# Adding the scan's carried states with one full-width product instead of four quarter-width products

## The reference, cut to what matters

```python
def step(h, inp):
    dt_t, B_t, C_t, x_t = inp
    dA = jnp.exp(dt_t[..., None] * A)
    h = dA * h + (dt_t * x_t)[..., None] * B_t[:, None, :]
    y = jnp.einsum('bdn,bn->bd', h, C_t)
    return (h, y)
h0 = jnp.zeros((B, D_INNER, D_STATE), xc.dtype)
_, ys = jax.lax.scan(step, h0, scan_xs)
```

## Time and profile before

| | us |
|---|---|
| median of 3 runs | 711.44 |
| lowest, highest | 710.73, 712.69 |
| the profiled execution, its own time | 711.19 |
| span of its instructions | 709.3 |
| TensorE busy in the span | 644.8 |
| VectorE, ScalarE, GpSimd busy | 551.7, 403.5, 385.7 |
| mean granted TensorE clock | 0.98 |

### The profile page before, as it was taken

One profiled execution on the slowest core, in us unless ns is written; L12 is line 12 of the kernel. 1 busy time (PEld: TensorE's weight loads), 2 busy tenths in 40 slices (PEclk: granted clock), 3 DMA queues, 4 the chain that ended last, 5 costly groups with the idle time before them and its releaser, 6 DMA issues.

```text
span 709.3 us, 25399 instructions
## 1 busy us (share of the span) xinstructions
PE 644.8 (91%) x11476; PEld 447.5 (63%) x11476; DVE 551.7 (78%) x466; ACT 403.5 (57%) x794; POOL 385.7 (54%) x140
## 2 busy tenths in 40 slices
PE   1989986999988999899999999999898999999997
PEld 1333342588977889788888889954345555565532
DVE  5599668489988989799899989963759787892345
ACT  1434789898877677677778767502247345324100
POOL 1000246779988789889899898963101143533000
PEclk9999999999999999999999999999989999999999
DMA  7980053420064110431340100015039899760202
GB/s 213 82 66 5 29 153 125 144 63 19 19 141 132 35 48 19 126 89 52 108 117 20 48 18 19 5 35 182 0 84 199 177 249 222 163 117 2 56 3 119
DMA packets 72627, 62.12 MB, mean 88 GB/s; under 512 B 34024, under 2 KB 57576, under 8 KB 72520
## 3 DMA queue, kind: packets, MB, share of 16 engines
q1 hardware_dynamic: 71560, 60.09, 36.9%
q10 hardware_dynamic: 960, 0.41, 0.2%
HBM read 44.22 MB, written 15.25 MB: 84 GB/s over the span
## 4 chain that ended last, share of the span: by engine, by line
PE 66%; POOL 11%; ACT 10%; DVE 7%; issue 4%; DMA 1%; SPq 0%; POOLq 0%; ACTq 0%; DVEq 0%
PE PS L1219 21%; PE PS L1338 8%; PE PS L1452 6%; POOL X L573 5%; PE PS L1241 5%; PE PS L1103 5%; PE PS L1436 4%; POOL arena L573 3%; POOL WIN L573 3%; PE PS L1267 2%; PE PS L1356 2%; PE PS L1238 2%; PE PS L1317 1%; ACT arena L837 1%; DMA X<-in_x 1%
## 5 line engine op out<-in xcount | busy, mean ns | idle before, releaser
L573 POOL TENSOR_TENSOR X<-X,spare 128x2048 f32<-128x2048 f32 x32 | 146.6, 4584 | 20.5 <-DVE X L1688 10.6
L1219 PE MATMUL PS<-mid,arena 128*32 128x128 f32 x4096 | 137.8, 273 | 6.6 <-issue 5.6
L1219 PEld LDWEIGHTS PS<-mid,arena 128*32 128x32 f32 x4096 | 121.6, 110 | 19.0 <-issue 13.2
L1219 PE MATMUL PS<-APROD,arena 128*32 128x128 f32 x2048 | 129.5, 273 | 3.1 <-issue 3.0
L1219 PE MATMUL PS<-WPR,arena 128*32 128x128 f32 x2048 | 128.9, 273 | 3.5 <-issue 1.3
L1219 PEld LDWEIGHTS PS<-WPR,arena 128*32 128x32 f32 x2048 | 110.7, 110 | 14.7 <-issue 6.9
L1219 PEld LDWEIGHTS PS<-APROD,arena 128*32 128x32 f32 x2048 | 111.2, 110 | 2.6 <-issue 2.2
L837 ACT ACTIVATE arena<-arena,small 128x512 f32<-128x512 f32 (+1 forms) x150 | 99.4, 711 | 18.4 <-DVE X L1688 10.0
L598 POOL TENSOR_TENSOR arena<-arena,PWR 128x512 f32<-128x512 f32 x30 | 42.7, 1454 | 70.6 <-PE PS L1338 70.5
L573 POOL TENSOR_TENSOR arena<-arena,spare 128x2048 f32<-128x2048 f32 x16 | 73.4, 4585 | 10.1 <-ACT mid L845 6.0
L573 POOL TENSOR_TENSOR WIN<-WIN,spare 128x2048 f32<-128x2048 f32 x16 | 73.3, 4583 | 7.1 <-DVE WIN L1688 5.0
(11 more groups left out here) (201 smaller groups left out, 1183.6 us busy)
## 6 DMA issues: line engine op xcount, KB each, us to landing
arena<-dt_rows SPq DMA_DIRECT2D x56, 256.0 KB, 3.8
arena<-patch_rows SPq DMA_DIRECT2D x40, 324.0 KB, 6.0
patch_rows<-arena SPq DMA_DIRECT2D x10, 648.0 KB, 7.2
X<-in_x SPq DMA_DIRECT2D x4, 1024.0 KB, 7.6
dt_rows<-arena SPq DMA_DIRECT2D x8, 512.0 KB, 2.6
spare<-c_rows SPq DMA_DIRECT2D x64, 64.0 KB, 2.2
tap_rows<-WPR SPq DMA_DIRECT2D x24, 88.0 KB, 7.7
mid<-dt_rows SPq DMA_DIRECT2D x8, 256.0 KB, 3.8
```

Of the source, the lines that this page charges most:

```text
L573: pool.tensor_tensor(HB[s % 4], HB[s % 4], CROW[:, k % 2:k % 2 + 1, :].broadcast_to([P, QN, HALF]), ALU.mult).then_inc(S["g_rd"], 1)
L1219: mm = pe.matmul(PS[32 * n:32 * n + 32, 4 + i, j * P:(j + 1) * P], DXT[:, DT_ * b + g, 4 * h + j, 32 * i:32 * i + 32], DIAGB[k % 2][n][:, ...
```

## The change

In every half-step with `h = 1`, the four quarter-width products at line 1223 become one product with the whole 128-column identity as the stationary operand, into all 128 partitions of the same column. The order, the waits and the semaphore stay.

```diff
                         if h and j == 0 and i % 2:
-                            for n in range(QN):
-                                pe.matmul(PS[32 * n:32 * n + 32, 4 + i, 0:1], IDENT[:, 32 * n:32 * n + 32], CARRY[:, DT_ * b + g, nq, i:i + 1], start=False, stop=True)
+                            pe.matmul(PS[:, 4 + i, 0:1], IDENT, CARRY[:, DT_ * b + g, nq, i:i + 1], start=False, stop=True)
                 mm.then_inc(S["u_ps"], 1)
```

## The result

The changed kernel is slower: 723.65 us at the median (four runs, 722.98 to 727.99) against 712.07 us for the kernel before (four runs, 710.73 to 713.27). The ratio is 1.0153, with a 95% interval of 1.0114 to 1.0192. By the medians it takes 11.6 us more. The forecast was 725.0 us, with 718 to 733 as its range. The profiled execution took 724.27 us, with a span of 722.4 us against 709.3.

The account below looks back on a forecast made before the run. TensorE was taken to drive the loop with a few per cent of room; A +6.2 and B +7.3 us sum to +13.5, on 711.19 us 724.7, and 0.25 below the median gives 725.0 us, range 718 to 733.

Parts of the forecast that it names:

- The price: TensorE's added path per half-step with h = 1: 0.45 us added less 0.06 removed, 0.39 us.
- distance of starts: Time from the last quarter product before line 1223's product to the first after it: 0.17 + 0.39 = 0.56 us.
- dense half-step: One block of inputs and one state sum in a dense piece of TensorE's timeline: 2.24 us before, near 2.63 predicted.
- The three pieces: Parts of the added product's cost: into full width 0.20 us, second pass 0.11, back to quarter width 0.14.
- The gain of 9.6 us: Skill-rule estimate at line 1223: 8 passes 0.2 us, 2 passes 0.05, so 0.15 us gained per place.
- The room: TensorE's time beyond dense work in the two h = 1 stretches, 10.3 and 6.1 us, claimed to be used up.
- A and B: The two h = 1 stretches, 219.39 to 304.88 us and 384.84 to 465.75 us; predicted growth 6.2 and 7.3 us.
- the pure path: TensorE's dense work plus 12.5 us per stretch: at least 87.7 us in A, 87.3 in B.
- Rival 1: None of TensorE's room in A and B is usable: +25.0 us, 736.4 us; chance 0.10 for above 733.
- Rivals 2 and 3: 2: product costs about half, room takes it, below 718 us, chance 0.16; 3: width changes free, 707.6 us, chance 0.04.
- The waits inside blocks: TensorE standing still inside blocks where the code has no wait; 4.0 us in A and 0.9 in B kept whole.
- The stretches with h = 0: Parts the change does not touch, one between A and B; predicted to stay, counted at nothing.

Follow-up runs that it names:

- halves: Changed kernel with two products of 64 stationary columns each in place of the one of 128; 714.82 us, ratio 1.0047.
- twice: Changed kernel with its full-width product issued twice in a row; 733.56 us, ratio 1.0293.
- behind: Changed kernel with pieces reordered, so the full-width product comes 0.9 us after its column was written; 722.18 us, ratio 1.0159.
- eight sets: Kernel before with its four quarter-width products issued eight times in a row; 807.18 us, ratio 1.138.
- with two sets: Kernel before with its four quarter-width products issued twice in a row; 720.2 us, ratio 1.0099.

## Why the prediction was right, and where it was not

*The price.* Predicted 0.39 us per half-step with h = 1, distance of starts 0.56, dense half-step 2.63. Measured: distance 0.53, half-step 2.63. The three pieces taken from far parts of the trace add up. The experiments bear out the parts: a pass is 0.11 us, the load is its content (halves), and the rest is paid once per change (twice), not for the column (behind). The Trainium skill, "TensorEngine Tiling (Array Packing)", section Key Properties, had it that a change of tiling mode drains the engine; the trace agrees, by 0.53 us in place of 0.11 where the width changes.

The gain of 9.6 us, which the prediction estimated by the rule of about 60 cycles per small product in the Trainium skill, the same page, section Instruction Overhead, did not come. One of its terms was formed wrongly: it put all 8 quarter-width passes one behind the other, 0.2 us, though quarters run side by side. Two passes per quarter would be 0.05 us by the same rule, and 0.06 was measured. The other term fails: a further one-column pass at full width took 0.11 us (the product issued twice), not 0.025.

*The room.* Predicted that TensorE alone would set the pace and its room be used up. It is: A and B are at 88.6 and 87.1 us, and the pure path was put at 87.7 and 87.3. (By the rounded terms of the prediction the dense work of A is 75.1 us and not 75.2, which changes nothing.) Rival 1 (nothing of the room usable, 736 us) is out. Rivals 2 and 3 are out by the price. As predicted, the other engines wait longer: VectorE for TensorE's inputs 10.6 us in A (8.5 before) and 10.2 in B (5.5), GpSimd for the scan 18.6 us in A (12.0) and 13.5 in B (7.3).

*The waits inside blocks: the step that failed.* I kept 4.0 us of them in A and 0.9 in B "whole". In the changed kernel they are 0.5 and 0. So A and B together grew by 9.3 us and not by 13.5. They are waits for TensorE's instructions, and the change relieved the supply twice: 12 records fewer per half-step, and 0.39 us more time for them. The kernel before used 160 records per dense half-step of 2.24 us, 71 per us, so a block of 256 lasted 3.6 us there. The changed kernel uses 148 in 2.63 us, so a block lasts 4.5 us. With eight sets, where TensorE waited for nearly every block, one came every 3.8 to 3.9 us. Over all of A it is 4875 records in 88.6 us, 55 per us, and was 5252 in 85.5, 61. The prediction had the price of the change right and called its one benefit nothing.

*The stretches with h = 0.* Predicted to stay. In the first profile they took 4.4 us more, which hid the 4.2 us that A and B fell short of. So the span's 13.1 us came close to the 13.5 forecast in part by luck; the medians differ by 11.6. In the second profile of the same kernel the first of them took 85.2 us, 0.2 less than before the change, and the second 1.8 more. In the second stretch the waits for blocks of instructions explain most of it: 2.0 us before, 4.4 and 3.2 in the two profiles of the changed kernel. Why these waits vary, and whether the change makes them longer there, stays open; nothing was tried on it.

*The resolution.* I took 0.3% as what can be told from no change. In two sets of 17 runs the kernel before lay between 707.4 and 715.7 us and between 707.8 and 716.1, so a single run tells little under 1%. The result is clear of that; the intervals, not single runs, carry the comparisons above.

## What to carry to other kernels

Do not count instructions when the tile width changes: one 128-column product among 32-column ones cost 0.45 us of path where eight passes of four quarter-width products cost 0.06. Price such a change from other transitions in the same trace, comparing ends of records, and read the load apart from the emptying. Where TensorE issues many tiny instructions, count its records per us as well: near 65 per us they were a bound of their own, which no engine's busy share shows. Its sign is an idle time put down to `issue` that begins at a block of 256 of its records.

## What the runs showed that was not expected

TensorE's supply of instructions held at 64 to 69 loads and products per us: 5771 in 90.7 us and 5752 in 86.8 us with two sets, 8840 in 135.9 and 8822 in 128.5 us with eight. It was the lower of the two in A each time, where the DMA engines were also busier (share 0.26 against 0.07, and 0.18 against 0.05). That a busier DMA lowers it fits these four values, but no run varied it alone, and with eight sets the transfers of the `instruction` queue were not longer in A (1.12 us on average) than in B (1.17). By the medians, a second set of quarter products cost 4.2 us beyond its path (8.2 - 4), and taking the only set out gained 3.0 us beyond it (6.8 - 3.8).
